# Who issues the adjacency loads, a rolled ScalarE loop, and the order around a block's end in a fused two-layer graph network kernel

## What is computed

```python
# layer 0: graph attention
Wh = h @ W;  f1 = Wh @ a1;  f2 = Wh @ a2
e = leaky_relu(f1 + f2.T, 0.2)
att = softmax(where(adj > 0, e, -9e15), axis=-1)
x = x + relu(att @ Wh)
# layer 1: K = 16 heads, weighted per node
node = h @ W1
hw = einsum('nc,kcf->nkf', h, W2)
x = x + relu(adj @ einsum('nk,nkf->nf', node, hw) + node @ b)
```

## Time and profile before

| | |
|---|---|
| median of 3 runs | 1799.24 us |
| profiled execution, its own time | 1796.01 us |
| its span, first to last instruction | 1794.4 us |
| mean granted TensorE clock | 0.985 of full speed |
| setup, up to the first weights' matmuls | 0 to 84 us |
| block 0 | 84 to 204 us |
| blocks 1 to 7 | 204 to about 1277 us |
| gather | to 1794 us |

### The profile page before, as it was taken

The page is one execution under the profiler, slowest core; times in us unless marked ns, Lnnn a source line. Parts: engine busy times, 40 slices in busy tenths (PEclk is TensorE's granted clock), DMA queues, the critical chain, the costliest instruction groups (busy, mean ns, idle before and its releaser), DMA issues.

```text
span 1794.4 us, 35785 instructions
## 1 busy us (share of the span) xinstructions
PE 1711.5 (95%) x11302; PEld 1477.7 (82%) x11302; DVE 1291.0 (72%) x1775; ACT 1088.0 (61%) x1889; POOL 553.1 (31%) x522
## 2 busy tenths in 40 slices
PE   5799899999989999998999999999899999999998
PEld 3599889879879888897897898888677788888886
DVE  5589788888878888887887887888656543443534
ACT  3555466756666666766766766665465655555554
POOL 0000035435445454354354453454634300000000
PEclk8899999999999999999999999999999999999999
DMA  9899999999999999999999999995723444444430
GB/s 217 205 339 364 349 285 302 300 277 305 309 278 307 305 292 296 299 308 275 303 310 287 292 308 301 278 304 216 296 110 150 147 165 174 163 180 162 164 140 23
DMA packets 316786, 452.50 MB, mean 252 GB/s; under 512 B 21072, under 2 KB 291616, under 8 KB 298912
## 3 DMA queue, kind: packets, MB, share of 16 engines
q1 hardware_dynamic: 158400, 222.33, 42.3%
q10 hardware_dynamic: 151472, 209.87, 40.5%
q0 software_dynamic: 6832, 19.41, 3.2%
HBM read 364.46 MB, written 87.07 MB: 252 GB/s over the span
## 4 chain that ended last, share of the span: by engine, by line
PE 79%; DMA 6%; ACTq 4%; ACT 4%; issue 3%; DVE 2%; POOL 1%; POOLq 0%; DVEq 0%
PE ot_ps L822 39%; PE mt_ps L879 13%; PE ot_ps L879 13%; PE hw_ps L791 11%; ACTq L294 4%; DMA maskT_d<-mt 2%; ACT wh_mask L530 2%; DMA xt<-in_x_dram 2%; DMA adj_sb<-in_adj_dram 1%; ACT prod L601 1%; DVE p_sb L1011 1%; PE h_ps L786 1%; PE hw_ps L721 1%; DMA keep_d<-keep 1%; POOL prod L404 1%
## 5 line engine op out<-in xcount | busy, mean ns | idle before, releaser
L822 PEld LDWEIGHTS ot_ps<-wh_mask,p_sb 128*128 128x128 f32 x8192 | 950.8, 194 | 95.6 <-issue 60.7
L822 PE MATMUL ot_ps<-wh_mask,p_sb 128*128 (+1 forms) x8192 | 960.1, 278 | 36.4 <-DVE p_sb L1011 32.1
L1011 DVE SCALAR_TENSOR_TENSOR p_sb<-zb,qcol,mt 128x1024 f32<-128x1024 uint8 (+1 forms) x512 | 727.9, 1437 | 21.0 <-DVE mt L935 10.0
L530 ACT ACTIVATE wh_mask<-adj_sb 128x2048 uint8<-128x2048 f32 x256 | 486.0, 1923 | 110.7 <-issue 77.1
L404 POOL TENSOR_TENSOR prod<-prod 128x1024 f32<-128x1024 f32 (+2 forms) x192 | 335.5, 1748 | 596.2 <-ACT prod L601 569.0
L1058 DVE CAST mask<-adj_sb 128x1024 fp32r<-128x1024 uint8 x272 | 204.0, 757 | 244.3 <-PE mt_ps L879 242.3
L628 ACT ACTIVATE mask<-adj_sb 128x1024 fp32r<-128x1024 uint8 x240 | 255.2, 1064 | 173.6 <-PE ot_ps L879 173.5
L601 ACT ACTIVATE prod<-hw_ps,node 128x128 f32<-128x128 f32 x1024 | 278.7, 383 | 113.1 <-PE hw_ps L791 111.7
L879 PE MATMUL mt_ps<-mask,msgs 128*128 128x512 f32 x1024 | 282.6, 398 | 2.0 <-DVE mask L1058 1.1
L879 PE MATMUL ot_ps<-mask,msgs 128*128 128x512 f32 x1024 | 274.7, 390 | 0.8
L791 PE MATMUL hw_ps<-wcat,hT 128*128 128x512 f32 x512 | 240.7, 592 | 0.0
(11 more groups left out here) (108 smaller groups left out, 565.6 us busy)
## 6 DMA issues: line engine op xcount, KB each, us to landing
adj_sb<-in_adj_dram SPq DMA_DIRECT2D x512, 256.0 KB, 7.8
adj_sb<-in_adj_dram ACTq DMA_DIRECT2D x512, 256.0 KB, 9.3
maskT_d<-mt ACTq DMA_DIRECT2D x64, 1024.0 KB, 10.5
adj_sb<-maskT_d SPq DMA_DIRECT2D x32, 2048.0 KB, 7.8
keep_d<-keep POOLq DMA_DIRECT2D x64, 128.0 KB, 6.1
p_sb<-keep_d SPq DMA_DIRECT2D x4, 2048.0 KB, 12.2
msg_d<-msg POOLq DMA_DIRECT2D x56, 128.0 KB, 5.8
msgs<-msg_d SPq DMA_DIRECT2D x7, 1024.0 KB, 8.9
```

The lines of the kernel that those rows point to most:

```text
L530: ins = act.activation(m8[:, q // 2, 2 * (q % 2) + part, :], adj_sb[:, q, part * T * COLS:(part + 1) * T * COLS], ACT.Copy, scale=EDGE)
L822: ins = pe.matmul(ot_ps[h][:, (t - t0) * ROW:(t - t0 + 1) * ROW], p_sb[:, r, t * P:(t + 1) * P], rows, start=begin and t == t0, stop=end a ...
L1011: dve.scalar_tensor_tensor(p_sb[:, r, :], zbf[:, bass.ds((ib % 2) * BLK, BLK)], qcol[:, bass.ds(tile + b_, 1)], mtb[:, p, k // 2, :, 2 * ( ...
```

## The change

All 8 loads of a buffer are issued by SyncE, quadrants in the order 0, 2, 1, 3. ScalarE issues none, and its loop over jg is a loop again (`whole` is gone). `start_weights` makes four weights (k = 0 and 1) before the denominators, where it made two. In the setup the five casts stand two steps later (behind steps 2 to 6). Of PE's idle matmuls, four now stand ahead of the matmul L770, and nine, where four stood, behind it.

```diff
         def load_adj(ib, jg, p, h):
-            load_quadrants(sp, ib, jg, p, h, (0, 1))
+            load_quadrants(sp, ib, jg, p, h, (0, 2, 1, 3))
@@ attention_loop
-                if alone or whole or not finish:
+                if alone or not finish:
                     turn(ib * IT, ib, 0, finish, False)
-                if whole:
-                    for jg in range(1, IT - 1):
-                        turn(ib * IT + jg, ib, jg, finish, False)
-                else:
-                    with eng.Fori(1 if alone or not finish else 0, IT - 1) as jg:
-                        turn(ib * IT + jg, ib, jg, finish, False)
+                with eng.Fori(1 if alone or not finish else 0, IT - 1) as jg:
+                    turn(ib * IT + jg, ib, jg, finish, False)
@@ scalar, setup
                 take_wh(i)
-                if i < 4:
-                    load_upper(0, 0, i)
-                if i < 5:
-                    cast(i // 2, i % 2, 1, 0)
-                if i in (3, 5):
-                    load_upper(0, 1, (i - 3) // 2)
+                if 2 <= i < 7:
+                    cast((i - 2) // 2, i % 2, 1, 0)
...
-            load_upper(0, 1, 2)
@@ scalar, turn
-                        if k == 1:
-                            load_upper(ib, jg + 1 + p, 3 - 2 * p)
-                        if k == 3:
-                            load_upper(ib, jg + 2, 2 * p)
...
-            attention_loop(act, turn, whole=True)
+            attention_loop(act, turn)
@@ tensor, setup
             pe.transpose(h_ps[0:2, 0:P], ext[:, :], ident[:, :]).then_inc(setup_pe, 1)
+            idle_run(4)
             pe.wait_ge(setup_dve, 6)
             pe.matmul(h_ps[:, HB // 2:HB // 2 + 2], ones[0:2, :], extd[:, :], start=True, stop=True)\
               .then_inc(setup_pe, 1)
-            idle_run(4)
+            idle_run(9)
@@ vector
-                        weighed = p == 0 and k == 0 and isinstance(jg, int) and jg == 0
+                        weighed = p == 0 and k < 2 and isinstance(jg, int) and jg == 0
...
-                for b_ in range(2):
-                    weigh(NB * ib, IT * ib, ib, 0, 0, b_, 0)
+                for k in range(2):
+                    for b_ in range(2):
+                        weigh(NB * ib, IT * ib, ib, 0, k, b_, 2 * k)
```

More of the change, by code:

```diff
@@ L241, in build @@
         past_sp = sem("past_sp")
-        past_act = sem("past_act")
         block = ctx.enter_context(nc.Block())
@@ L262, in ends_block, with attention_loop @@
             return isinstance(jg, int) and jg == IT - 1
-        def attention_loop(eng, turn, start_block=None, end_block=None, alone=False, whole=False):
+        def attention_loop(eng, turn, start_block=None, end_block=None, alone=False):
             def one_block(ib, finish, last):
@@ L515, in take_wh @@
                                    ot_ps[g][:, 0:(t1 - t0) * (D + 2)], ACT.Copy).then_inc(wh_copied, 1)
-            def load_upper(ib, jg, q):
-                if jg >= IT:
-                    ib, jg = ib + 1, jg - IT
-                if isinstance(ib, int) and ib == NB:
-                    return
-                if not (isinstance(ib, int) and ib == 0 and jg == 0):
-                    act.wait_ge(adj_cast[q], ib * IT + jg)
-                load_quadrants(act, ib, jg, q // 2, q % 2, (2, 3))
             def cast(q, part, count, squared_before):
```

## The result

| | before | after |
|---|---|---|
| median of 20 runs | 1799.15 us (1792.59 to 1804.96) | 1787.39 us (1756.20 to 1829.69) |
| profiled execution, its own time | 1796.0 us | 1774.9 us |
| span | 1794.4 us | 1773.3 us |

The changed kernel scatters by 4%, the kernel before by 0.7%, at like granted clocks (0.98 to 0.99). The forecast was 1735 us: the range and the sign held, the size did not, 12 us on the medians where 64 were forecast.

What follows compares the result with a forecast made beforehand. TensorE (PE), busy 95% of the span, was taken as the bound, with gains only where it waits: 1796.0 - 20.7 (setup) - 10 (block 0 to 1) - 33 (block ends) = 1732.3, + 3.2 for the median: 1735 us, range 1718 to 1812.

Steps and rivals of the forecast that it cites:

- Setup: Setup: with the first cast behind step 2, the last normalising starts 20.7 us earlier; bounds of the gain 14 and 22.
- Idle matmuls: Setup, around L770 and L775: small delays against PE kept working ahead of L775; taken as 0, bounds -1.8 and +1.5.
- Block 0: Block 0's 8 half-turns: PE and load limits both near, loads now in one queue; taken as 0, bounds -4 and +12.
- Block ends and block 0 to 1: PE's waits at ends of blocks 1 to 6 shrink, -33 us (bounds -20 and -35); at block 0 to 1, -10.
- SyncE: SyncE issues 16 loads per half-turn instead of 8, within its waiting time; priced at 0 in blocks 1 to 7.
- The DMA engines: Loads in one alternating queue: rate between 204 and 349 GB/s, taken near the upper end, cost 0; below 231 loads bound.
- Rival 3: Loads half in step, 280 GB/s in all: +62 us, block 0 +12, about 1800 us (1765 to 1812); chance 0.10.
- rival 1: ACT's loop jumps still stall: 23 us given back, 1758; with the inner jump too, 1781 us; chance 0.16.
- Rival 2: Alternating loads stay in step at 204 GB/s, 20.5 us per half-turn: +71, 1870 us, up to 2030; chance 0.18.

Runs made afterwards that it cites:

- e3: Kernel before with four weights computed ahead and the later setup casts moved two steps later, both queues still loading: 1801.1 us, ratio 1.001.
- e4: Kernel before with all loads moved to SyncE (order 0, 2, 1, 3) and ScalarE's short loop, casts and two weights as before: 1813.4 us, ratio 1.005.
- after_again: The changed kernel itself, unaltered, run ten more times on another chip: 1794.9 us, ratio 0.999 to the kernel before.
- e1: Kernel before with four instead of two weights computed ahead of the old sums, nothing else: 1803.8 us, ratio 1.002.
- e10: Changed kernel with GpSimd storing `keep` ahead of its fold and awaiting the message store only behind the next fold: 1756.2 us, ratio 0.972 to the kernel before.
- e6: Changed kernel with ScalarE's four turns of a block written out again, without loads: 1775.0 us, ratio 0.986 to the kernel before.
- e5: Changed kernel with the loads in the order 0, 1, 2, 3 in SyncE's queue: 1831.3 us, ratio 1.016 to the kernel before.

## Why the prediction was wrong, point by point

- **Setup, -20.7:** measured -17.1, within the bounds of 14 to 22. The mechanism was only part of it: later casts without the loads' move gave 3 us (e3), the loads' move without the casts 8.6 (e4), both with the idle matmuls 17.1. The step on the setup saw the cast's wait of 15.42 us and not the issues behind it, which take its place.
- **Idle matmuls, 0:** not separated. The granted clock of the setup rose from 0.86 to 0.95, and the four passes that took 3.59 us take 1.98. It lies inside the setup's 17.1.
- **Block 0, 0 with bounds -4 and +12:** measured +12.5 in this execution, 18.5 in after_again and 31 in e4, which issues the same loads. This is the first step that failed. It asked whether the engines stay in step and answered for the upper end. A rate in between is what the traces show: 286 GB/s of loads in the median, and 235 to 304 in other executions of that order. A half-turn of 14.3 us needs 4.19 MB / 14.3 = 293 GB/s of loads beside the stores; one of 18.1 needs 231. So the same queue is too slow in block 0 and fast enough afterwards. The upper bound of 12 was itself too low, as it took 31 MB at 300 instead of 347 GB/s, a rate that holds the stores too, where only loads count.
- **Block ends and block 0 to 1, -33 and -10:** the first half-turns of blocks 1 to 6 gave 5.4 us each, 32.3 in all, block 7's 4.2. The sum for block 1's start was lost again in front of it: the last half-turn of block 0 went from 18.8 to 26.9 us, since the sums now wait for a late load's cast. The working took weights and deviation as two parts of one sum; e1 and e4 show that neither pays in full alone (+5 and -21 beside the -36.5 us of both).
- **SyncE, 0:** right in blocks 1 to 7, with 116.6 us left of its 767 us of waiting for casts.
- **The DMA engines, 0 in blocks 1 to 7:** right but for one late load in block 6 (about 6 us), by e10's 312 GB/s. Rival 3 had the rate (280) and the +12 in block 0, and its "about 1800" (its own terms give 1799 + 62 + 12 - 64 = 1809) lies near the medians of 1787 and 1795. That nearness is luck, as is that of rival 1's 1781, whose stall did not come: the 1.1 us per half-turn of rival 3 did not come either. It let the mask stores share the 280 GB/s, and the humps of over 400 show that they run on top.
- **What no step had:** the ordinary half-turn. The chain there was TensorE's work alone, and the forecast took that as a guarantee for the changed kernel. It put the half-turn's term at nothing, and it was not said how near the next loop was. GpSimd's fold, cut, store and `kept` had 11 us of waits in 3 places before; it took 87 us more of GpSimd's time and became the bound. The 49 half-turns grew by 19.6 us, about 6 of them the late load of block 6, and fell by 28 to 32 once the loop was cut (e10). This is the costliest miss.
- **Rival 1** fell: no issue gap ahead of a cast inside the blocks. In e6 a loop over written-out turns did not stall either; with the load issues in it, it did (e1). The Trainium skill, Runtime: NRT & Kernel Launch, "Instruction fetch mechanics", puts the stall down to a jump out of a window of instructions; the length of the code deciding, and not the jump, agrees with that, and so do the 56 packets of the instruction queue against 25, while its advice of full unrolling gained nothing that was shown here; e6 followed it within a block only. **Rival 2** fell: nothing ran at 204 GB/s for long; its nearest relative, e5, ran at 220. The Trainium skill, SBUF — State Buffer, "Can I just issue two DMAs to hit both halves?", gives two transfers to both halves 6% over one; the traces here disagree, with 346 GB/s from two queues beside 220 one-sided.
- **The sums:** the range of the forecast, 1718 to 1752, does not come out of the bounds named for its terms (14 to 22, -1.8 and +1.5, -4 and +12, -20 and -35), which give 1726 at the low end and about 1768 at the high end. 4.19 MB at 8 x 27.2 GB/s are 19.3 us, not 19.2.

## What to carry to other kernels

A chain that is one engine's work alone says that it is the bound, not by how much: before taking time from an engine's waits, measure the length of each other loop in the steady state (here fold, store, landing, `kept`, VectorE, over two half-turns) and ask whose work ran in the pauses that go. Price a moved transfer against each stage's own need, since one rate was enough at 18.1 us and too little at 14.3. And test parts of a change in pairs: the weights without the loads' move gave nothing, the move without the weights cost time, and together, with the later casts, they gained. A rate that is read from one execution is not yet a price: the single queue's went from 235 to 304 GB/s.

## What was not expected of the hardware

- One queue with loads that alternate between the halves of the partitions moved 262 to 285 GB/s of loads in the kernel after, and 235 to 304 in the median of block 0 from one execution to the next; the same loads in one-sided pairs 220, two queues with a half each 346. From 110 to 150 us the DMA shares were between 1.08 and 1.11 in the kernel before, the kernel after and e5.
- Mask stores came on top of that: 430 GB/s in the slices in which they ran beside loads at 262.
- GpSimd's addition of 128 x 256 took 722 to 732 ns beside a VectorE at rest and 1583 to 1799 beside one of VectorE's weights. A weight took up to 3.5 us beside the long addition of the fold (3.1 in the kernel before), and 1.3 with GpSimd at rest.
- An issue on ScalarE took 0.58 us in the middle of blocks, and 2.9 us in the setup of e3 (three in 8.73 us); the DMA engines were busy all the time in both places.
- Loads whose source pattern has four entries in its outermost dimension kept the sixteen DMA engines 25.5% busy: 3595 us for the whole kernel.
